# Splitting the Gram product and the output projections of a macaron block into high and low parts

## The reference, cut to what matters

```python
x = x + 0.5 * ffn(layernorm(x))
x = x + attn(layernorm(x))
x = x + 0.5 * ffn(layernorm(x))
def ffn(x):                       # x_prev: the token before, 0 at the start
    xr = mu_r * x + (1 - mu_r) * x_prev
    xk = mu_k * x + (1 - mu_k) * x_prev
    return sigmoid(xr @ W_r) * (square(relu(xk @ W_k)) @ W_v)
def attn(x):                      # 16 heads of 16
    q, k = relu(x @ Wq) / 4, relu(x @ Wk) / 4
    v, u = x @ Wv, silu(x @ Wu)
    out = q @ (k.T @ v)           # per head, over all tokens of a sequence
    return (srms_norm(out) * u) @ Wo
```

## Time and profile before

| | |
|---|---|
| median of 3 runs | 328.40 us (328.38 to 328.44) |
| profiled execution | 328.15 us, its span 326.3 us |
| busy: PE / PEld | 317.1 us (97%) / 282.9 us (87%) |
| busy: DVE / ACT / POOL | 236.2 us (72%) / 226.3 us (69%) / 167.2 us (51%) |
| granted TensorE clock | 1.000 over the whole span |

### The profile page before, as it was taken

How to read it: one execution, slowest core, us unless ns; L and a number is a source line. 1 busy time by engine, 2 the same in 40 slices (tenths; PEclk the granted TensorE clock), 3 DMA queues, 4 the chain that set the end, 5 groups by cost and what they waited for, 6 DMA issues and landing times. The chain is left out here.

```text
span 326.3 us, 5493 instructions
## 1 busy us (share of the span) xinstructions
PE 317.1 (97%) x1932; PEld 282.9 (87%) x1932; DVE 236.2 (72%) x560; ACT 226.3 (69%) x443; POOL 167.2 (51%) x195
## 2 busy tenths in 40 slices
PE   6898999999999999999999999999999999999996
PEld 6676898889889988988988998989999999989885
DVE  3689984594665736865774688475979999989744
ACT  3699957848839558569239346459797969588861
POOL 4297855625438238246227016015285959585560
DMA  7960000000000000000000000000001020111103
GB/s 228 349 198 0 3 1 0 2 0 2 0 1 3 0 0 2 0 2 0 0 3 1 2 0 0 2 0 2 1 2 64 2 66 0 66 65 64 50 18 129
DMA packets 11035, 10.83 MB, mean 33 GB/s; under 512 B 768, under 2 KB 11008, under 8 KB 11008
## 3 DMA queue, kind: packets, MB, share of 16 engines
...
q10 hardware_dynamic: 576, 0.26, 0.3%
...
## 5 line engine op out<-in xcount | busy, mean ns | idle before, releaser
L727 DVE SCALAR_TENSOR_TENSOR mix<-psA,mu,mix 128x512 f32<-128x512 f32 x64 | 44.1, 744 | 13.2 <-ACT mix L472 13.0
L336 POOL TENSOR_TENSOR mix_k_lo<-mix,mix_k_hi 128x512 fp32r<-128x512 f32 x30 | 39.5, 1335 | 13.3 <-ACT mix_k_hi L490 13.3
L472 ACT ACTIVATE mix<-psA,one_mu 128x511 f32<-128x511 f32 x64 | 39.5, 697 | 2.0 <-PE psA L1004 2.0
L987 PE MATMUL psRV<-ffn_hi,mix_r_hi 128*128 128x256 f32 x128 | 36.4, 284 | 0.0
L989 PE MATMUL psRV<-ffn_hi,mix_r_lo 128*128 128x256 f32 x128 | 35.7, 279 | 0.0
L988 PE MATMUL psRV<-ffn_lo,mix_r_hi 128*128 128x256 f32 x128 | 35.7, 279 | 0.0
L459 ACT ACTIVATE xn<-xs,shiftA,rstdA 128x256 f32<-128x256 f32 x59 | 30.8, 605 | 1.8 <-POOL shiftA L320 1.8
L747 DVE TENSOR_TENSOR mix_r_lo<-mix,mix_r_hi 128x512 fp32r<-128x512 f32 x30 | 27.5, 956 | 4.9 <-ACT mix_r_hi L490 4.9
L549 ACT ACTIVATE q_store<-psX 128x512 f32<-128x512 f32 x16 | 9.6, 598 | 29.2 <-PE psX L989 29.2
L1155 PE MATMUL psX<-wo,g_t 128*128 128x256 f32 x128 | 28.9, 379 | 0.0
L1100 PE MATMUL psK<-k_tok,xs 128*128 128x256 f32 x128 | 28.9, 379 | 0.0
...
## 6 DMA issues: line engine op xcount, KB each, us to landing
...
```

Source lines behind the costliest of these rows:

```text
L336: nc.gpsimd.tensor_tensor(mix_k_lo[:, h, :], mix[:, 0, h, :], mix_k_hi[:, h, :].bitcast(F32), ALU.subtract).then_inc(s_lo_k, 1)
L472: nc.scalar.activation(mix[:, rk, h, 1:BLOCK], psA[:, h, 0:BLOCK - 1], ACT.Copy, scale=one_mu[:, rk, h:h + 1]).then_inc(s_prev, 1)
L727: nc.vector.scalar_tensor_tensor(out=m, in0=psA[:, h, :], scalar=mu[:, rk, h:h + 1], in1=m, op0=ALU.mult, op1=ALU.add).then_inc(s_mix, 1)
L987: nc.tensor.matmul(dst, a_hi, b_hi, start=start, stop=False)
```

## The change

Seven of the eight Gram products (blocks 1 to 7) and all eight output projections become split products. For that ScalarE makes high parts of x1 (`x1_high`, 1024 columns), of k (`kt_high`, two pieces of 512 columns) and of Wo, and writes g's copy out of PSUM as its high part; GpSimd makes the low parts of x1 (`x1_low`), k (`kt_low`) and Wo; VectorE makes g's low part (`g_low`) from PSUM. Beside the second FFN GpSimd makes r's low parts up to step 13, VectorE those of 14 and 15 as before; `project_out(j)` follows `ffn_v(n)` for n = 8 to 11, and with it `add_attention` moves to the next step's start. Two large tiles (`silu_u`, `q_store`) become rings of five blocks to make room.

```diff
+            def r_low(n):
+                for h in range(HALVES):
+                    pool.wait_ge(s_hi_r, 2 * n + h + 1)
+                    nc.gpsimd.tensor_tensor(mix_r_lo[:, h, :], mix[:, 1, h, :], mix_r_hi[:, h, :].bitcast(F32),
+                                            ALU.subtract).then_inc(s_lo_r, 1)
...
+            def x1_low(a):
+                for g in range(2):
+                    pool.wait_ge(s_x1hi, a)
+                    nc.gpsimd.tensor_tensor(x1_lo[:, g * BANK:(g + 1) * BANK], row(xs, a, g * BANK, BANK),
+                                            x1_hi[:, g * BANK:(g + 1) * BANK].bitcast(F32),
+                                            ALU.subtract).then_inc(s_x1lo, 1)
+            def kt_low(a):
+                for g in range(2):
+                    pool.wait_ge(s_kt_hi, 2 * (a - 1) + g + 1)
+                    tiles = slice(2 * g, 2 * g + 2)
+                    nc.gpsimd.tensor_tensor(k_lo[:, tiles, :], k_tok[:, tiles, :], k_hi[:, tiles, :].bitcast(F32),
+                                            ALU.subtract).then_inc(s_kt_lo, 1)
...
-            for i in range(1, 5):
+            for i in range(1, 6):
                 act_low(i)
                 k_low(i + 1)
+                if i > 1:
+                    kt_low(i - 1)
                 scales_a(i + 2)
                 scales_b(i)
+                x1_low(i)
...
             act_low(7)
+            kt_low(6)
             scales_b(7)
             scales_a(9)
             norm_second(2)
+            x1_low(7)
+            kt_low(7)
             k_low(8)
             scales_a(10)
...
                     k_low(n + 1)
+                    r_low(n + 1)
                     if n > 8:
                         add_ffn2(n - 1)
...
+            def x1_high(a):
+                act.wait_ge(s_x1, 2 * (a + 1))
+                act.wait_ge(s_gt, a)
+                nc.scalar.activation(x1_hi[:], row(xs, a), ACT.Identity).then_inc(s_x1hi, 1)
+            def kt_high(a, g):
+                act.wait_ge(s_kt, 4 * a + 2 * g + 2)
+                tiles = slice(2 * g, 2 * g + 2)
+                nc.scalar.activation(k_hi[:, tiles, :], k_tok[:, tiles, :], ACT.Identity).then_inc(s_kt_hi, 1)
...
-                for t in range(1, TILES):
-                    sigmoid_u(i - 1, t)
+                sigmoid_u(i - 1, 1)
+                if i > 1:
+                    kt_high(i - 1, 0)
+                sigmoid_u(i - 1, 2)
+                sigmoid_u(i - 1, 3)
+                if i > 1:
+                    kt_high(i - 1, 1)
...
+                x1_high(i)
...
                 relu_q(i - 1)
...
+            def g_low(j):
+                for h in range(HALVES):
+                    dve.wait_ge(s_g, 2 * j + h + 1)
+                    nc.vector.tensor_tensor(g_lo[:, h, :], psX[:, h, :], g_hi[:, h, :].bitcast(F32),
+                                            ALU.subtract).then_inc(s_g_lo, 1)
...
             x2_low(6)
             projections(6)
+            g_low(1)
             for g in range(2):
                 gate_ffn(7, g)
                 add_ffn1(7, g)
...
+                    if a > 0:
+                        pe.wait_ge(s_x1lo, 2 * a)
...
+                        if f == 0 and t % 2 == 0:
+                            pe.wait_ge(s_kt_lo, 2 * (a - 1) + t // 2 + 1)
+                        rows = slice(t * D + f * P, t * D + (f + 1) * P)
+                        last = product(dst, x1_hi[:, rows], x1_lo[:, rows], k_hi[:, t, :], k_lo[:, t, :],
+                                       t == 0, t == TILES - 1)
...
                     attend(j + 1, [(s_relu, 2 * (n + 1))])
+                    ffn_v(n)
                     project_out(j)
-                    ffn_v(n)
```

More of the change, by code:

```diff
@@ L385, in _ @@
             scales_a(1)
-            for h in range(HALVES):
-                pool.wait_ge(s_hi_r, h + 1)
-                nc.gpsimd.tensor_tensor(mix_r_lo[:, h, :], mix[:, 1, h, :], mix_r_hi[:, h, :].bitcast(F32),
-                                        ALU.subtract).then_inc(s_lo_r, 1)
+            r_low(0)
             act_squares(0)
@@ L431, in _ @@
                     k_low(n + 1)
+                    if n == 12:
+                        r_low(n + 1)
             add_ffn2(14)
@@ L624, in _ @@
             sigmoid_r(7, 1)
-            for t in range(1, TILES):
-                sigmoid_u(6, t)
+            sigmoid_u(6, 1)
+            kt_high(6, 0)
+            sigmoid_u(6, 2)
+            sigmoid_u(6, 3)
+            kt_high(6, 1)
             keep_g_rows(1)
@@ L917, in _ @@
                 projections(i - 1)
+                if i == 6:
+                    g_low(0)
                 gate_ffn(i, 0)
@@ L947, in _ @@
             projections(7)
+            g_low(2)
+            gate_heads(3)
             r_low(8)
-            gate_heads(3)
             add_attention(2)
@@ L959, in _ @@
                     gate_ffn(n - 1, 1)
+                    add_attention(j - 1)
                 head_norms(j)
@@ L963, in _ @@
                 mix_current(n + 1, (0,))
+                g_low(j)
                 mix_current(n + 1, (1,))
@@ L966, in _ @@
                     gate_heads(j + 1)
-                    add_attention(j)
-                r_low(n + 1)
             for n in range(13, LAST):
@@ L1150, in project_out @@
             def project_out(j):
[L1151 to L1152 removed]
+                if j < SPLIT_O:
+                    pe.wait_ge(s_wo_lo, 1)
+                    pe.wait_ge(s_g_lo, 2 * j + 2)
+                else:
+                    pe.wait_ge(s_g, 2 * j + 2)
                 for t in range(TILES):
+                    dst = psX[:, t // 2, (t % 2) * D:(t % 2 + 1) * D]
                     for c in range(HALVES):
[L1155 to L1156 removed]
+                        if j < SPLIT_O:
+                            last = product(dst, g_hi[:, c, tok(t)], g_lo[:, c, tok(t)], wo_hi[:, c, :],
+                                           wo_lo[:, c, :], c == 0, c == HALVES - 1)
+                        else:
+                            last = nc.tensor.matmul(dst, g_t[:, c, tok(t)], wo[:, c, :],
+                                                    start=(c == 0), stop=(c == HALVES - 1))
                     if t % 2:
```

74 lines of the change are left out of this document (50 added, 24 removed).

## The result

| | before | after |
|---|---|---|
| median of 4 runs each | 328.39 us (328.10 to 328.44) | 322.57 us (322.11 to 323.19) |
| ratio, 95% interval | | 0.9826 (0.9808 to 0.9843) |
| profiled execution, span | 328.15, 326.3 | 323.19, 321.5 |
| busy PE / PEld | 317.1 / 282.9 | 309.6 / 280.2 |
| busy DVE / ACT / POOL | 236.2 / 226.3 / 167.2 | 239.8 / 239.7 / 215.0 |

The forecast was 323.3 us, 4.85 under the profiled execution of before. The profiled execution of after is 4.96 under that of before.

A forecast was written before the change was run, and what follows sets the result against it. The prediction took TensorE, busy 97% of the span, as the bound end to end. It summed 328.15 - 9.3 - 0.4 + 0.5 + 0.25 + 1.05 + 0.95 + 0.6 + 1.55 = 323.3 us, range 320.0 to 326.0.

The forecast's parts named there:

- 9.3 for the products: Seven Gram products and eight projections as split products on TensorE, each saving 0.62 us, 9.3 us in all.
- The estimate of 0.94 us per product by four passes: Alternative saving per product, counting four passes of 0.118 us for true float32; sum 14.2 us, not adopted.
- 0.4 for the old waits: Steps 10 to 12: extra time in the transposes of g goes as the head norm starts sooner, 0.4 us saved.
- +0.5 in steps 2 to 4, for keep_g: VectorE's add meets GpSimd's low part of k, ends 0.55 later, delaying keep_g; 0.15 us a step, 0.5 in all.
- +0.25 in step 7: g_low(1) ahead of gate_ffn moves VectorE's chain by 0.85, so q waits for add_attention(1); 0.25 us lost.
- +1.05 for gram(7): Between steps 7 and 8, TensorE waits for block 7's k parts, 0.95 us for the low part plus 0.1.
- +0.95 and +0.6 in steps 10 and 11: Small VectorE head-norm instructions wait for GpSimd's add_ffn2, making act_low2 and W_v late; 0.95 and 0.6 us lost.
- +1.55 in steps 12 and 13: GpSimd's low parts of step 13 hold ScalarE's previous(14), so mix_high(14) comes late; 1.55 us lost.
- A: Rival, chance 0.22: the small instructions in steps 10 and 11 don't wait for GpSimd; 320.7 us.
- B: Rival, chance 0.13: first half less covered, ScalarE or GpSimd lateness costs some 0.4 in six Gram products; 325.7 us.
- D: Rival, chance 0.02: the new products are not cheaper, each costing 3.6 us; 334.9 us.
- C: Rival, chance 0.05: GpSimd sets the step from 10 on, at 17.5 us, and the kernel is slower; 330.0 us.

The follow-up runs named there:

- chain_psum: Changed kernel with the small head-norm instructions of blocks 3 to 7 keeping data in PSUM, one instruction more; 320.23 us, ratio 0.9779 to the kernel before.
- short_add: Changed kernel with GpSimd's second-FFN additions (add_ffn2) in steps 9 to 11 cut from 512 to 4 columns; 320.21 us, ratio 0.9769 to the kernel before.
- the lock kernel: Separate kernel timing VectorE's 64-column instructions beside idle or busy GpSimd (lock: one waits for the other's end); SBUF-to-SBUF tensor_scalar 0.193 to 0.721 us beside subtractions.
- r13_vector: Changed kernel with r's low part of step 13 alone given back to VectorE; 321.79 us, ratio 0.9825 to the kernel before.

## Why the prediction was right

**The body went from 309.11 to 304.27 us, by 4.84, and the sum was 4.85.** So close a total is luck. The table has the errors, measured less forecast: -0.43 in steps 2 to 4, +0.09 in 5 and 6, -0.07 in 7, -0.01 in 8 and 9, +0.14, +0.09 and +0.20 in 10, 11 and 12 with 13. One term of 0.5 that was not there paid for several that were too small. Here they are one by one.

- *9.3 for the products.* Right to a few hundredths each: 2.82 us for a projection and 2.86 to 2.88 for most Gram products, against 2.83. Steps 8 and 9 gained 0.62 and 0.63, steps 2 and 3 gained 0.59 and 0.58. The estimate of 0.94 us per product by four passes was too high, because it priced a pass at the 0.118 us of an fp32r matmul. In a row of float32 matmuls a group of two (four records) takes 0.86 or 0.87 us, so 0.43 each, and a quarter of that is 0.108. The runs speak against that price, not against four passes. The groups are the kernel's last, after the change:

```profile
315.69 1.03 PE L1146 MATMUL psX<-ffn_v_plain,act_k 128*128 128x256 f32 x4
316.55 1.03 PE L1146 MATMUL psRV<-ffn_v_plain,act_k 128*128 128x256 f32 x4
```

- *0.4 for the old waits.* In the changed kernel it can't be told apart, as new waits stand in the same place. chain_psum has it: its transposes of g take 0.87 us in steps 10 to 12, against 1.10, 1.01 and 1.00 before, and its steps 10 and 11 are 14.82 long, where the forecast for TensorE alone was 14.84.
- *+0.5 in steps 2 to 4, for keep_g.* **This term failed**: those steps fell short of 3 x 0.62 by 0.03. The meeting was real, but it held the add for 0.45 instead of 0.55, and a tenth of that was taken up by idle time behind it. keep_g ended 21.17 us into step 3, 0.37 later than before, and the next step began at 21.37 with no wait. Two tenths of error in a chain with no slack on paper was the whole term.
- *+0.25 in step 7.* Attend took 0.13 over its 1.70, and little else shows; this and the next term together came to 1.23 where 1.30 was forecast.
- *+1.05 for gram(7).* Measured 1.05, of which 0.92 is the wait and 0.13 the product's place behind transposes, which the forecast had not.
- *+0.95 and +0.6 in steps 10 and 11.* Measured, against 14.82, 1.11 and 0.74; chain_psum and short_add give both back to the hundredth. W_v was held by GpSimd's act_low2 until 10.17 us, where 10.1 was forecast; what made the term too small is that TensorE was there at 9.08 and not at 9.2. The end of the chain was forecast at 5.95 us and came at 6.01, though one reason in it was wrong. I let the tensor_scalar pass and held the instruction behind it. The trace shows the tensor_scalar itself held (1.19 us), so that the end comes out the same. The Trainium skill (SBUF — State Buffer, Who interferes with whom) lists that operation among the contenders, which I had not drawn on; the lock kernel agrees, 0.193 to 0.721.
- *+1.55 in steps 12 and 13.* They lost 1.03 where the forecast had TensorE able to gain 0.75: 1.78. It has two parts. ScalarE's previous(14) came 16.8 us into the step, by the forecast mechanism; without it the two steps are 0.88 (r13_vector) to 1.00 us (short_add) shorter, where 0.8 was forecast. The other 0.8 to 0.9 is the gain that TensorE never gets, in any of the kernels, since it waits for ScalarE's xn instead. That the 0.75 would be lost was right; I had put it down to mix_high(14) and had not seen the wait for xn. The late head norm of step 12 (transposes of g of 1.29 us instead of 0.87) costs only 0.1, as the wait for xn takes up the rest.

**The rivals.** A, no wait for the small instructions, is out for this kernel: they waited. Its price, 2.6 us under the forecast, is what chain_psum measured when it made A true: 2.73 in the body, 2.62 in the medians of one chip. B and D are out by step 3: no wait of TensorE there, and products of 2.86. C is out by chain_psum: with the same work, GpSimd let steps of 14.82 through. Only the lock stood behind steps 10 and 11, so C would have needed several such meetings on the path, and there was one.

Not tried was what would be left if gram(7)'s low part were ready in time without moving q, nor an earlier xn for step 14.
